# Differential attention with a quantised gate: where the exponentials are kept, the order of maxima and combination, and the steps of the gate product

## The chip, the cores and the metric

The kernel runs on one core of one Trainium2 chip. The metric is the device time of one execution in microseconds. Engine names are those of the profile: PE is TensorE (PEld its weight loads), DVE is VectorE, ACT is ScalarE, POOL is GpSimd, SP is SyncE, whose queue issues all transfers here.

## The reference, cut to what matters

The input is x of shape (8, 512, 512). It is normalised, and two things are computed from it: a differential attention with 8 pairs of query heads over 4 pairs of key heads, and a gate, which is SiLU of a product whose operands are rounded to a 4-bit block format. The output is x + attention * gate.

```python
xn = layernorm(x)
q, k, v = split(xn @ Wqkv.T + b)            # 16 q heads, 8 k heads of 128; 4 v of 256
p = softmax_causal(q1 k1) - lam * softmax_causal(q2 k2)
o = (p @ v) * rsqrt(mean((p @ v)**2) + eps) * subln_w * (1 - lambda_init)
s = o @ out_w.T + out_b
g = silu(quant(xn) @ quant(W_ffn).T + b_ffn)
x = x + s * g
```

## The kernel before

**Steps.** After a setup (weights transposed and split) the kernel goes through 8 batches (b) of 512 tokens, each in 32 steps (s); n = 32 b + s counts all 256. A step is one pair of query heads on one block of 128 tokens, with w = 128, 256, 384 or 512 keys: s % 8 = 0, 1 have 128; 2, 3 have 256; 4, 5 have 384; 6, 7 have 512. Eight steps share a group g of keys and values. Every product is made of three matmuls on float16 pairs (a high part and a remainder), so each result is split by two operations: ACT writes the high part, DVE the remainder.

**A step's own chain.** `scores(n)` on PE (6 matmuls of w columns) fills two rows of PSUM, m = 1 and m = 0. `maxima(n, m)` on DVE scales and masks a row in place and gives its bound. `exps(n)` on ACT takes the two exponentials: that of m = 1 stays in PSUM, that of m = 0 goes to `pp` in SBUF. `combine(n)` on DVE (reciprocal, coefficient, product) forms p in PSUM; `p_hi(n)` on ACT and `p_lo(n)` on DVE write `ph`; `transpose_p(n)` on SP's queue turns it into `pT` by a DMA transpose; `attend(n)` on PE multiplies by v. Then `square_o` (ACT), `norm_of` (POOL), `normalised` (ACT), `normalised_lo` (DVE) and `transpose_o` (SP) bring the head into `heads`.

**Fills.** Between `scores(n + 2)` and `attend(n)` PE computes what `PLAN[n]` lists: a projection q, k (12 matmuls of 512 columns) or v (24 of 256), the output product "out" of the batch before (48 of 512, in steps 1, 3, 5, 7), and the gate product "ffn" (4 of 512, in steps 10 to 13). Two PSUM banks hold them in turn (`fill_free` returns a bank). A q or k fill is split by ACT, then DVE (L658, L940); a v fill goes DVE (L946), ACT (L663), POOL (`v_low`, L1138); an ffn fill DVE (L952), ACT's tanh (L669), POOL (`gating`, L1150 and L1152). In the last batch the output product of its own first two blocks is cut in pieces ("last"), from step 22 on, which hold one bank.

**Order.** Each engine's program is an order written by hand: one iteration n per step. The iteration of each engine does:

- PE: `scores(n + 2)`, the fills of n, `attend(n)`.
- DVE: `combine(n + 1)`, `maxima(n + 2, 1)`, `p_lo(n + 1)`, `maxima(n + 2, 0)`, `normalised_lo(n - 1)`, the fills of n.
- ACT: `square_o(n - 1)`, `p_hi(n + 1)`, `normalised(n - 1)`, `exps(n + 2)`, the fills of n.
- SP: `transpose_p(n + 1)`, loads and the transposes of x (`X_TURN`, steps 21 and 22) and of the quantised x, `transpose_o(n - 1)`.

`scores(n)` may overwrite a pair of rows when `p_lo(n - 2)` has read it:

```python
wait(pe, ph_lo, n - 1)
```

In steps with `X_SPLIT` ACT and DVE also split a block of the next batch's x. In the steps after an "out" fill DVE does the maxima last.

Of the kernel before, what the change touches and what calls it, by code (L numbers as in the profile page):

```python
# [7 lines left out]
F32 = mybir.dt.float32  # L8
# [12 lines left out]
G = 4  # L21
# [19 lines left out]
PH = 4 - AHEAD  # L41
# [10 lines left out]
FFN_STEP = 10  # L52
# [17 lines left out]
def schedule(has_prev, has_next):  # L70

    steps = [[] for _ in range(NS)]
    for g in (1, 2, 3):

        at = (None, PROJ_AT, PROJ_AT[:6] + (7, 8), (0, 1, 1, 2, 3, 3, 4, 5))[g]
        for s, (kind, j) in zip(at, PROJ):
            steps[(g - 1) * STEPS + s].append((kind, g, j))
    for k in range(NT):
        if has_prev:
            steps[2 * k + 1].append(("out", 0, k))  # L80

        steps[FFN_STEP + k].append(("ffn", 0, k))
# [4 lines left out]
    else:  # L87
# [9 lines left out]
X_SPLIT = {15: 0, 17: 1, 18: 2, 19: 3}  # L97
# [78 lines left out]
def build(nc, x_d, wqkv_d, bqkv_d, lq1_d, lk1_d, lq2_d, lk2_d, sub_d, ow_d, ob_d, fw_d, fb_d, out_d):  # L176
# [4 lines left out]
    with ctx:  # L181
# [22 lines left out]
        pp = sb("pp", [P, S], F32)  # L204
# [3 lines left out]
        junk = sb("junk", [P, E], BF16)  # L208
# [10 lines left out]
        lam4, lam2 = pp, v32[:, 1, :]  # L219
# [46 lines left out]
        ld_bias = sem("ld_bias")  # L266
        ld_w = [sem(f"ld_w{n}") for n in range(16)]
# [43 lines left out]
        tanh_one = sem("tanh_one")  # L311
        gate_done = sem("gate_done")
# [54 lines left out]
        def _(sp):  # L367
# [65 lines left out]
            for n in range(NSTEPS):  # L433
# [18 lines left out]
                if s == 0 and b:  # L452
                    sp.wait_ge(xT_done[1], 16 * (b + 1))
# [29 lines left out]
        def _(pe):  # L483
# [48 lines left out]
            def scores(n):  # L532
# [6 lines left out]
                wait(pe, ph_lo, n - 1)  # L539
# [27 lines left out]
            for kind, n in setup_order():  # L567
# [20 lines left out]
                for c in range(4):  # L588
                    last = tr(setup_bank(m)[:, c * P:(c + 1) * P], slot(kind, n // 2)[:, n % 2, c * P:(c + 1) * P], ident[:])
# [20 lines left out]
        def _(act):  # L610
# [42 lines left out]
            def fill(f):  # L653
# [17 lines left out]
            def exps(n):  # L671
                u, w = n % 2, place(n)[3]

                wait(act, eps_done, n - 5)
                for a, m in enumerate((1, 0)):
                    act.wait_ge(max_done, 2 * n + a + 1)
                    sc = sc_ps[u][:, m, 0:w]
                    if m == 0:

                        wait(act, comb_done, n)  # L680
                    run(sc if m else pp[:, 0:w], sc, ACT.Exp, bias=ebias[:, u, m:m + 1], scale=-1.0,  # L681
                        accum_out=psum_l[:, n % 6, m:m + 1]).then_inc(exp_done, 1)

            def p_hi(n):
# [5 lines left out]
                run(ph[:, n % PH, 0:w], sc_ps[u][:, 1, 0:w], ACT.Copy, scale=sigma).then_inc(ph_hi, 1)  # L690
# [539 lines left out]
```

## Time and profile before

| | us |
|---|---|
| median of 3 runs | 1753.76 (1753.6 to 1755.99) |
| the profiled execution's own time | 1754.4 |
| its span, first to last instruction | 1752.6 |
| PE busy in the span | 1538.7 (88%) |
| DVE, ACT, POOL busy | 1196.0 (68%), 885.8 (51%), 662.4 (38%) |
| batch 5, from the end of the last attend of batch 4 to that of batch 5 | 200.48 |

The span is split below by the ends of `attend(n)` on PE. Matmuls overlap, and a matmul's printed duration is longer than the time from its start to that of the next; so the length of a stretch says more than PE's busy share in it. Of a pair of rows on one engine, the distance of the starts is the time that the first one takes from the engine. "PEclk" is the clock granted to PE as a share of the full one. An idle time in brackets is that of the engine just before the row, with what ended it.

### The profile page before, as it was taken

What the parts mean: (1) busy time and instruction counts of PE and PEld (TensorE: products, weight loads), DVE (VectorE), ACT (ScalarE), POOL (GpSimd) and SP (SyncE); (2) the same over time, 40 slices, a digit from 0 to 9 for tenths busy, and PEclk for the clock granted to TensorE, in tenths of its full rate; (3) what the DMA queues carried; (4) which work ended last, traced back from release to release, by engine and by line L of the source; (5) the groups of instructions that cost most, each with busy time, mean ns of one, the idle gap of its engine ahead of it and who ended that gap; (6) DMA issues with size and microseconds to landing.
All of it is one profiled execution on the core that took longest, in us unless ns stands there. A gap on an engine that the chain in (4) does not pass through costs nothing. (4 is left out here: it accounts for less than half of the span.)

```text
span 1752.6 us, 28521 instructions
## 1 busy us (share of the span) xinstructions
PE 1538.7 (88%) x9137; PEld 899.8 (51%) x9153; DVE 1196.0 (68%) x3177; ACT 885.8 (51%) x2542; POOL 662.4 (38%) x1161
## 2 busy tenths in 40 slices
PE   2666588999989988999889988999989989899898
PEld 1343355555555555545555555545555546555554
DVE  4467777776777677776677667775777767675682
ACT  4563356535663456535664356634564356533561
POOL 2103542345324443344424443244424443243433
PEclk7778799999999999999999999999999999999999
DMA  7401334333342334333352334324342333422433
GB/s 250 140 4 27 64 67 82 61 88 70 50 91 55 84 73 82 64 78 72 55 87 57 84 73 79 68 46 100 55 85 54 95 63 65 80 54 67 64 76 73
DMA packets 385353, 130.63 MB, mean 75 GB/s; under 512 B 366354, under 2 KB 366900, under 8 KB 385204
## 3 DMA queue, kind: packets, MB, share of 16 engines
q1 hardware_dynamic: 385204, 128.81, 35.4%
q8 instruction: 73, 1.20, 0.3%
q14 instruction: 76, 0.62, 0.1%
HBM read 31.74 MB, written 8.39 MB: 23 GB/s over the span
## 5 line engine op out<-in xcount | busy, mean ns | idle before, releaser
L690 ACT ACTIVATE ph<-ps,small 128x128 f16<-128x128 f32 (+3 forms) x256 | 134.4, 525 | 395.0 <-DVE ps L981 394.4
L1168 POOL TENSOR_SCALAR norm<-psum_l,small 128x1 f32<-128x1 f32 x256 | 88.4, 345 | 584.9 <-ACT pp L681 584.9
L970 DVE CUSTOM_DVE_ANT_0 ps<-ps,mask,ssc 128x384 f32<-128x384 f32 (+3 forms) x512 | 279.7, 551 | 35.9 <-PE ps L547 35.4
L490 PE MATMUL ps<-xT,wqkv 128*128 128x512 f16 x768 | 297.6, 387 | 6.8 <-DVE qkv L940 6.4
L491 PE MATMUL ps<-xT,wqkv 128*128 128x512 f16 x768 | 296.4, 386 | 0.0
L492 PE MATMUL ps<-xT,wqkv 128*128 128x512 f16 x768 | 295.5, 385 | 0.0
L940 DVE SCALAR_TENSOR_TENSOR qkv<-ps,bsc,qkv 128x512 f16<-128x512 f32 x192 | 143.3, 750 | 187.0 <-ACT qkv L658 187.0
L490 PE MATMUL ps<-qkv,pT 128*128 128x256 f16 x640 | 179.6, 281 | 74.3 <-DMA pT<-ph 73.5
L545 PE MATMUL ps<-qkv 128*128 128x384 f16 (+3 forms) x512 | 155.2, 309 | 56.5 <-DVE ph L987 53.6
L490 PE MATMUL ps<-wout,heads 128*128 128x512 f16 x512 | 194.1, 379 | 0.5 <-DVE small L956 0.5
L491 PE MATMUL ps<-wout,heads 128*128 128x512 f16 x512 | 194.0, 379 | 0.0
L492 PE MATMUL ps<-wout,heads 128*128 128x512 f16 x512 | 194.0, 379 | 0.0
L987 DVE SCALAR_TENSOR_TENSOR ph<-ps,small,ph 128x128 f16<-128x128 f32 (+3 forms) x256 | 141.0, 551 | 77.2 <-ACT ph L690 68.6
L702 ACT ACTIVATE on<-ps,norm 128x256 f16<-128x256 f32 x256 | 120.5, 471 | 132.7 <-POOL norm L1176 130.0
L492 PE MATMUL ps<-qkv,pT 128*128 128x256 f16 x640 | 180.3, 282 | 0.0
L491 PE MATMUL ps<-qkv,pT 128*128 128x256 f16 x640 | 179.7, 281 | 0.0
L993 DVE SCALAR_TENSOR_TENSOR on<-ps,norm,on 128x256 f16<-128x256 f32 x256 | 123.1, 481 | 66.8 <-ACT on L702 66.5
L1174 POOL TENSOR_TENSOR var<-norm,sumsq 128x1 f32<-128x1 f32 x256 | 65.1, 254 | 246.7 <-ACT junk L694 246.6
L546 PE MATMUL ps<-qkv 128*128 128x384 f16 (+3 forms) x512 | 155.4, 309 | 0.0
L547 PE MATMUL ps<-qkv 128*128 128x384 f16 (+3 forms) x512 | 155.3, 309 | 0.0
L681 ACT ACTIVATE pp<-ps,ebias 128x128 f32<-128x128 f32 (+3 forms) x256 | 135.0, 527 | 37.0 <-DVE ebias L970 35.9
L1176 POOL TENSOR_TENSOR norm<-var,small 128x1 f32<-128x1 f32 x256 | 143.6, 561 | 20.0
(147 smaller groups left out, 3146.9 us busy)
## 6 DMA issues: line engine op xcount, KB each, us to landing
xin<-in_L_attn_hidden_states SPq DMA_DIRECT2D x8, 1024.0 KB, 5.8
xres<-in_L_attn_hidden_states SPq DMA_DIRECT2D x32, 256.0 KB, 2.8
out_x<-res SPq DMA_DIRECT2D x32, 256.0 KB, 2.4
qkv<-in_L_attn_Wqkv_w SPq DMA_DIRECT2D x8, 512.0 KB, 7.3
heads<-in_L_attn_Wqkv_w SPq DMA_DIRECT2D x8, 512.0 KB, 10.7
pT<-ph SPq DMA_TRANSPOSE x256, 2.7
heads<-on SPq DMA_TRANSPOSE x256, 2.5
qkv<-in_L_attn_out_w SPq DMA_DIRECT2D x4, 512.0 KB, 5.6
```

The lines of the kernel that those rows point to most:

```text
L490: mm(out, ah, bh, start=start and j == 0, stop=False)
L491: mm(out, ah, bl, start=False, stop=False)
L492: last = mm(out, al, bh, start=False, stop=stop and j == n - 1)
L545: mm(out, qh, k[:, 0, m, 0:w], start=True, stop=False)
L546: mm(out, qh, k[:, 1, m, 0:w], start=False, stop=False)
L547: last = mm(out, ql, k[:, 0, m, 0:w], start=False, stop=True)
L681: run(sc if m else pp[:, 0:w], sc, ACT.Exp, bias=ebias[:, u, m:m + 1], scale=-1.0, accum_out=psum_l[:, n % 6, m:m + 1]).then_inc(exp_done, 1)
L690: run(ph[:, n % PH, 0:w], sc_ps[u][:, 1, 0:w], ACT.Copy, scale=sigma).then_inc(ph_hi, 1)
L940: stt(out=dst(kind, g, j, 1), in0=bank, scalar=bsc[:, g, c:c + 1], in1=dst(kind, g, j, 0), op0=ALU.add, op1=ALU.subtract).then_inc(fill_fr ...
L970: nc.vector.tensor_tensor_reduce(sc, sc, mask[:, S - w:S], ssc[:, c:c + 1], BIG, ALU.add, ALU.min, ebias[:, u, m:m + 1]).then_inc(max_done, 1)
L987: stt(out=ph[:, n % PH, w:2 * w], in0=sc_ps[u][:, 1, 0:w], scalar=sigma, in1=ph[:, n % PH, 0:w], op0=ALU.mult, op1=ALU.subtract).then_inc( ...
L1176: pt(nr[:, 1:2], var[:], minushalf, ALU.pow).then_inc(norm_done, 1)
```

## The change

- The exponential of m = 1 goes to SBUF as well: `pp` has three slices, 0 for m = 0 and 1 + n % 2 for m = 1. `combine` reads two slices and writes one, all in SBUF; `p_hi` and `p_lo` read SBUF. `scores(n)` waits for the two exponentials of step n - 2 instead of for `p_lo(n - 2)`.
- DVE does both maxima of step n + 2, then `combine(n + 1)` and `p_lo(n + 1)`. ACT does the exponential of m = 1 of step n + 2 ahead of `p_hi(n + 1)`, that of m = 0 after `normalised(n - 1)`. Steps after an "out" fill keep combination, remainder, fill, maxima on DVE.
- The ffn fills go from steps 10 to 13 to steps 22 to 25 and stand last in their step. DVE adds the bias in PSUM (`biased`), ACT takes the tanh out of PSUM into `gate`, and in its next iteration DVE (`gating`, one operation of 512 columns) multiplies, which returns the bank. POOL's two operations for it go.
- The two v fills of group 2 go from steps 15 and 16 to steps 14 and 15. The first split of the next batch's x goes from steps 15 and 17 to 14 and 16; its halves are kept in `gate` instead of `res`, `xres` and `aq`. The transposes of the quantised x stay at steps 10 and 11.
- The bias of v is loaded for each group in turn (a DMA of 256 floats to all partitions at every eighth step) instead of once, and its scale is applied in the fill: a scalar_tensor_tensor in place of a tensor_tensor.
- The junk output of `square_o` goes to PSUM. In the last batch SP loads the first residual after step 25 instead of 22.

```diff
-FFN_STEP = 10
+FFN_STEP = 22
-        at = (None, PROJ_AT, PROJ_AT[:6] + (7, 8), (0, 1, 1, 2, 3, 3, 4, 5))[g]
+        at = (None, PROJ_AT, PROJ_AT, (0, 1, 1, 2, 3, 3, 4, 5))[g]
...
-X_SPLIT = {15: 0, 17: 1, 18: 2, 19: 3}
+X_SPLIT = {14: 0, 16: 1, 18: 2, 19: 3}
...
+                if n and s % STEPS == 0 and n // STEPS + 1 < G * B:
+                    load_v(n // STEPS + 1)
...
-                wait(pe, ph_lo, n - 1)
+                wait(pe, exp_done, 2 * n - 2)
...
-                    act.wait_ge(fill_free, n + 1)
-                    wait(act, gate_done, f.gate)
-                    wait(act, v_lo, f.v)
-                    run(t2, gate[:, j, :], ACT.Tanh, scale=0.5).then_inc(tanh_done, 1)
+                    act.wait_ge(biased, f.gate + 1)
+                    wait(act, gated, f.gate - NT + 1)
+                    if f.gate // NT + 1 < B:
+                        act.wait_ge(xT_done[j], 16 * (f.gate // NT + 2))
+                    run(gate[:, j, :], bank, ACT.Tanh, scale=0.5).then_inc(tanh_done, 1)
...
+                if n + AHEAD < NSTEPS and not late:
+                    exps(n + AHEAD, 1)
                 if n + AHEAD - 1 < NSTEPS:
                     p_hi(n + AHEAD - 1)
...
-                stt(out=sc_ps[u][:, 1, 0:w], in0=sc_ps[u][:, 1, 0:w], scalar=coef[:, u:u + 1], in1=pp[:, 0:w],
+                stt(out=pp[:, 1 + u, 0:w], in0=pp[:, 1 + u, 0:w], scalar=coef[:, u:u + 1], in1=pp[:, 0, 0:w],
...
+            def gating(f):
+                dve.wait_ge(tanh_done, f.gate + 1)
+                stt(out=gate[:, f.j, :], in0=gate[:, f.j, :], scalar=1.0, in1=fbank[f.bank], op0=ALU.add, op1=ALU.mult)\
+                    .then_inc(fill_free, 1)
...
+                if n + AHEAD < NSTEPS and not late:
+                    maxima(n + AHEAD, 1)
+                if n + AHEAD < NSTEPS and not late:
+                    maxima(n + AHEAD, 0)
                 if n + AHEAD - 1 < NSTEPS:
                     combine(n + AHEAD - 1)
-                if n + AHEAD < NSTEPS and not late:
-                    maxima(n + AHEAD, 1)
-                if n + AHEAD - 1 < NSTEPS:
                     p_lo(n + AHEAD - 1)
...
+                for f in PLAN[n - 1] if n else ():
+                    if f.kind == "ffn":
+                        gating(f)
```

## Rows read from the trace of the kernel before

**Rows 1.** Waits of PE after the setup, 180 us to the end: us in total, times, longest.
```profile
PE ps L490 <- DMA pT<-ph: 73.5, 36, 3.9
PE ps L545 <- DVE ph L987: 37.7, 25, 11.4
```
**Rows 2.** Batch 5 by stage (steps 0-7, 8-13, 14-16, 17-21, 22-24, 25-31), from the view by windows.
```profile
1132.56:1207.86 75.30, 75.30 (x423) 40.63 (x421) 50.50 (x126) 27.68 (x77) 35.34 (x53) 1.00 0.31 70
1207.86:1238.71 30.85, 29.17 (x161) 15.35 (x162) 22.32 (x58) 18.78 (x54) 13.15 (x23) 1.00 0.36 76
1238.71:1257.05 18.34, 14.89 (x107) 11.16 (x105) 11.45 (x33) 10.23 (x32) 9.86 (x16) 0.81 0.37 58
1257.05:1284.24 27.19, 27.16 (x174) 16.68 (x173) 22.32 (x56) 17.74 (x49) 8.00 (x16) 1.00 0.27 50
1284.24:1298.99 14.75, 9.00 (x59) 5.80 (x57) 7.98 (x28) 7.81 (x29) 4.71 (x11) 0.88 0.77 143
1298.99:1333.04 34.05, 31.23 (x210) 19.29 (x208) 26.02 (x72) 20.77 (x63) 8.59 (x22) 1.00 0.40 65
```
**Rows 3.** The same view for step 9 of batch 5 alone.
```profile
1211.43:1215.00 3.57, 3.57 (x23) 2.00 (x21) 2.98 (x9) 1.72 (x6) 2.90 (x4) 1.00 0.20 41
```
**Rows 4.** DVE in order of time, one step of 512 keys with a q fill.
```profile
1319.22 0.15 DVE L977 RECIPROCAL recip<-psum_l 128x1 f32<-128x1 f32 x1
...
1320.38 0.75 DVE L970 CUSTOM_DVE_ANT_0 ps<-ps,mask,ssc 128x512 f32<-128x512 f32 x1
...
1321.23 0.75 DVE L987 SCALAR_TENSOR_TENSOR ph<-ps,small,ph 128x512 f16<-128x512 f32 x1
1321.90 0.75 DVE L970 CUSTOM_DVE_ANT_0 ps<-ps,mask,ssc 128x512 f32<-128x512 f32 x1
...
1324.13 0.75 DVE L940 SCALAR_TENSOR_TENSOR qkv<-ps,bsc,qkv 128x512 f16<-128x512 f32 x1 [1.09 <-ACT qkv L658]
1324.80 0.15 DVE L977 RECIPROCAL recip<-psum_l 128x1 f32<-128x1 f32 x1
```
**Rows 5.** ACT in the same step.
```profile
1320.51 0.69 ACT L690 ACTIVATE ph<-ps,small 128x512 f16<-128x512 f32 x1 [1.63 <-DVE ps L981]
1321.10 0.47 ACT L702 ACTIVATE on<-ps,norm 128x256 f16<-128x256 f32 x1
...
1322.74 0.69 ACT L681 ACTIVATE pp<-ps,ebias 128x512 f32<-128x512 f32 x1 [0.51 <-DVE ebias L970]
...
1323.42 0.68 ACT L658 ACTIVATE qkv<-ps,bsc 128x512 f16<-128x512 f32 x1
```
**Rows 6.** ACT in step 13 of batch 5, which has an ffn fill.
```profile
1235.55 0.63 ACT L669 ACTIVATE v<-gate 128x512 f32<-128x512 f32 x1 [2.30 <-DVE gate L952]
...
1236.45 0.68 ACT L690 ACTIVATE ph<-ps,small 128x512 f16<-128x512 f32 x1
```
**Rows 7.** A DVE split that reads SBUF alone, grouped by form: busy us, mean ns.
```profile
L1007 DVE SCALAR_TENSOR_TENSOR aq<-xin,aq 128x512 f16<-128x512 f32 x16 | 10.8, 682 | 0.0
```
**Rows 8.** DVE in order of time, two maxima in a row.
```profile
1151.08 0.62 DVE L970 CUSTOM_DVE_ANT_0 ps<-ps,mask,ssc 128x384 f32<-128x384 f32 x1 [0.51 <-PE ps L547]
...
1151.63 0.62 DVE L970 CUSTOM_DVE_ANT_0 ps<-ps,mask,ssc 128x384 f32<-128x384 f32 x1
```
**Rows 9.** DVE in order of time, the form of rows 7 in batch 2.
```profile
652.84 1.23 DVE L1007 SCALAR_TENSOR_TENSOR res<-xin,res 128x512 f16<-128x512 f32 x1 [1.21 <-ACT res L711]
```
**Rows 10.** POOL in the same stretch.
```profile
652.37 1.16 POOL L1138 TENSOR_TENSOR qkv<-v,qkv 128x512 f16<-128x512 f32 x1 [0.71 <-ACT qkv L663]
```
**Rows 11.** Issues of SP's queue, steps 22 and 23 of batch 5.
```profile
1288.49 1.26 SPq L410 DMA_TRANSPOSE pT<-ph  x1
...
1293.95 1.20 SPq L410 DMA_TRANSPOSE pT<-ph  x1
```
**Rows 12.** The transposes of p (L410) in steps 8 to 31 of batch 5, from issue to landing.
```profile
DMA to landing us min/median/max: 2.3/2.6/4.5
```

More of the change, by code:

```diff
@@ L40 @@
 AHEAD = 2
-PH = 4 - AHEAD
+PH = 2
 ROUND = (22 << 23) + (1 << 22)
@@ L92, in schedule @@
             steps[LAST_STEP + s].insert(0, ("last", p, k))
+    for k in range(NT):
+        steps[FFN_STEP + k].append(("ffn", 0, k))
     return steps
 PROLOGUE = [(kind, 0, j) for kind, j in PROJ]
-X_SPLIT = {15: 0, 17: 1, 18: 2, 19: 3}
+X_SPLIT = {14: 0, 16: 1, 18: 2, 19: 3}
 X_TURN = {21: (0, 1), 22: (2, 3)}
@@ L266, in build @@
         ld_bias = sem("ld_bias")
+        ld_vb = [sem(f"ld_vb{u}") for u in range(2)]
         ld_w = [sem(f"ld_w{n}") for n in range(16)]
@@ L396, in _ @@
                 load_w(n)
+            for k in range(NT):
+                sp.wait_ge(xT_done[k], 16)
             sp.dma_start(gate[:], fw_d.rearrange("(k p) h -> p k h", p=P)).then_inc(ld_fw, 16)
@@ L458, in _ @@
                         residual(b - 1, (s - 1) // 2)
-                if b == B - 1 and s == LAST_STEP:
+                if b == B - 1 and s == FFN_STEP + 3:
+                    sp.wait_ge(fill_done, fill_of("ffn", b, 0, 1) + 1)
                     residual(b, 0)
-                for k in {FFN_STEP - 1: (0, 1), FFN_STEP: (2, 3)}.get(s, ()):
+                for k in {10: (0, 1), 11: (2, 3)}.get(s, ()):
                     if k == 0:
@@ L664, in fill, with exps @@
                 elif kind == "ffn":
[L666 to L682 removed]
+                    act.wait_ge(biased, f.gate + 1)
[3 more added lines that the diff above has]
+                    run(gate[:, j, :], bank, ACT.Tanh, scale=0.5).then_inc(tanh_done, 1)
+            def exps(n, m):
+                u, w = n % 2, place(n)[3]
+                if m:
+                    wait(act, eps_done, n - 5)
+                    wait(act, ph_lo, n - 1)
+                else:
+                    wait(act, comb_done, n)
+                act.wait_ge(max_done, 2 * n + 2 - m)
+                out = pp[:, 1 + u, 0:w] if m else pp[:, 0, 0:w]
+                run(out, sc_ps[u][:, m, 0:w], ACT.Exp, bias=ebias[:, u, m:m + 1], scale=-1.0,
+                    accum_out=psum_l[:, n % 6, m:m + 1]).then_inc(exp_done, 1)
             def p_hi(n):
@@ L944, in fill @@
                     wait(dve, v_lo, f.v)
-                    wait(dve, gate_done, f.ffn)
-                    tt(v32[:], bank.rearrange("p (a e) -> p a e", a=2),
-                       vbias[:, g, :].unsqueeze(1).broadcast_to([P, 2, E]), ALU.add).then_inc(fill_free, 1)
+                    t = f.v // 2
+                    dve.wait_ge(ld_vb[t % 2], 16 * (t // 2 + 1))
+                    stt(out=v32[:], in0=vbias[:, t % 2, :].unsqueeze(1).broadcast_to([P, 2, E]), scalar=vscale[:, g:g + 1],
+                        in1=bank.rearrange("p (a e) -> p a e", a=2), op0=ALU.mult, op1=ALU.add).then_inc(fill_free, 1)
                 elif kind == "ffn":
                     dve.wait_ge(fill_done, n + 1)
-                    wait(dve, gated, f.gate - NT + 1)
-                    tt(gate[:, j, :], bank, fbias[:], ALU.add).then_inc(fill_free, 1)
+                    tt(bank, bank, fbias[:], ALU.add).then_inc(biased, 1)
                 elif kind == "last" and LAST_PIECES[j][g][1] < OC:
@@ L1056, in _ @@
                     fill(f)
-                if n + AHEAD < NSTEPS:
-                    if late:
-                        maxima(n + AHEAD, 1)
+                if n + AHEAD < NSTEPS and late:
+                    maxima(n + AHEAD, 1)
                     maxima(n + AHEAD, 0)
+                for f in PLAN[n - 1] if n else ():
+                    if f.kind == "ffn":
+                        gating(f)
                 prepare(b, s, "maxima")
@@ L1145, in _ @@
             v_low(0, 1, 1)
-            def gating(f):
-                pool.wait_ge(tanh_done, f.gate + 1)
-                pt(t2, t2, one.broadcast_to([P, HID]), ALU.add).then_inc(tanh_one, 1)
-                pool.wait_ge(tanh_one, f.gate + 1)
-                pt(gate[:, f.j, :], t2, gate[:, f.j, :], ALU.mult).then_inc(gate_done, 1)
             def finish(f):
@@ L1186, in _ @@
                 for f in PLAN[n - 1] if n else ():
-                    if f.kind == "ffn":
-                        gating(f)
-                    elif f.kind == "out" or f.kind == "last" and LAST_PIECES[f.j][f.g][1] == OC:
+                    if f.kind == "out" or f.kind == "last" and LAST_PIECES[f.j][f.g][1] == OC:
                         finish(f)
```

64 lines of the change are left out of this document (35 added, 29 removed).

## The prediction

> **What bounds the kernel now.** I read PE's waits first, to see which ones are worth anything, then the stages of one batch, then the order of time on DVE and ACT. PE is the engine with the most work, and behind the setup it waits for two things above all: transposed tiles p that land late (73.5 us) and `p_lo`, which frees the rows of the scores (37.7) [rows 1]. Step 9 shows what PE needs when it waits for nothing: 6 score matmuls, 24 halves of a k fill and 3 of attend, 33 units of 256 columns in 3.57 us, 0.108 each [rows 3]. By that unit the stages of a batch [rows 2] compare with their bare PE work so:
>
> - steps 0 to 7: 75.3 us without a gap; output products cover everything. What an engine does here costs nothing.
> - 8 to 13: 266 units, 28.8, took 30.85.
> - 14 to 16: 111 units, 12.0, took 18.34, at 0.81 of the clock: PE idled for 3.5 us and then ran part of the stage at the lower of its two levels.
> - 17 to 21: 249 units, 26.9, took 27.19: PE-bound.
> - 22 to 24: 63 units, 6.8, took 14.75.
> - 25 to 31: 279 units, 30.2, took 34.05.
>
> So 20 us of a batch of 200 are not PE's work. They stand where fills are thin (14, 22, 23) or where a loop through DVE and ACT is longer than PE's step. That loop can be read off one step [rows 4, 5]. Combination starts at 1319.22; p_hi starts at 1320.51, p_lo at 1321.23, the second maximum at 1321.90, its exponential 1322.74, the q fill's high part 1323.42, its remainder 1324.13, the next combination 1324.80: 5.58 us, against PE's 45 units (4.9). The first maximum lies under p_hi for nothing; the second is in the loop.
>
> **The loop after.** Both maxima come first. Two in a row start 0.55 apart at 384 columns [rows 8], so 0.67 each at 512, where a like DVE row takes 0.67 [rows 4]. Combination: 1.26 from its start to its end (1320.48, by p_hi's start less 0.03). Its operands are in SBUF then; the nearest row is a split reading SBUF alone, 0.682 [rows 7] against 0.75 for the PSUM one [rows 4], so I take 1.19. A bound from below is this, from above no gain, 1.26. p_hi to normalised 0.59, less about 0.05 for an SBUF source (the tanh out of SBUF takes 0.63, p_hi 0.68 [rows 6]): 0.54. Normalised to the exponential 0.36, as now to the first one, exponential to fill 0.68, to remainder 0.71, remainder 0.67 [rows 4, 5]. Sum 1.34 + 1.19 + 0.03 + 0.54 + 0.36 + 0.68 + 0.71 + 0.67 = 5.52 against 5.58. The maximum that was hidden is paid for (+0.67), but p_lo and the second maximum's wait leave the loop. Each 128 keys fewer take about 0.12 from each of five operations, 0.6, from either loop. So in steps with a q or k fill the new order by itself is worth about nothing. In steps with a v fill ACT's tail isn't in the loop and p_hi's wait, now uncovered, is: I count 4.9 at 512 keys and 4.5 at 384/512, about 0.5 more than before.
>
> **The gate product leaves steps 10 to 13.** Its bias (0.6 us of DVE) stood at the end of the loop and its tanh on ACT stood ahead of p_hi: it starts at 1235.55, p_hi only at 1236.45 behind it and the square [rows 6], so most of its 0.63 is in the loop too: 5.58 + 0.6 + 0.6 = 6.8 at 512 keys. After: loops of 4.3, 4.7, 4.9, 5.3 and 5.5 from step 9 on, beginning 4.7 us after the end of step 7 in both kernels (the k fill of step 8 sets it). Counting from the end of step 7, PE's work of 234 units is done at 25.3; p of step 13 is written 22.1 and lands 24.9, just late: stage 25.9 against 30.85, **-5.0**.
>
> **The v fills one step earlier.** Step 14 has work then. Loop 13 starts at 23.8, p of 14 lands 31.0 (4 us to p_lo's end, 3.2 transpose), PE is ready at 28.8: it idles 2.2 instead of 3.5, too short, I take it, for the clock to fall. p of 15 lands at 35.7, step 15 ends 37.0, step 16 (a single k) 40.6: 14.7 against 18.34, **-3.6**.
>
> **Steps 17 to 21.** The DVE loops (5.0, 5.3, 6.2, 4.5, 4.9 with splits of x and double fills) sum to 25.9, PE's work is 26.9. Bare PE work and 0.6 of waits: 27.5, **+0.3**.
>
> **Steps 22 to 24.** Three ffn fills add 24 units (2.6) where PE idles anyway, but the loops get ffn bias (0.6) and gating (0.67), and bank reuse now runs through DVE: an ffn fill waits for the gating of the one before, which stands behind the maxima, combination and p_lo. Counting on: step 21 ends 68.1; p of 22 lands 72.4, step 22 ends 73.8; p of 23 lands 77.8, since combination waits for `v_low` (next part), and step 23 ends 79.6 with some slow clock. Maxima start on the scores of 26 at 80.3, gating ends 83.2, ffn fill 84.1, step 24 ends 84.5, and tanh ahead of p_hi costs 0.5: 16.9 against 14.75, **+2.2**. SP is no better off: its two issues of p stand 5.46 apart here [rows 11], with four others between, and it gets one more short load at steps 8, 16 and 24, at most one transposing issue of 1.26, behind the transpose of p.
>
> **Steps 25 to 31.** One more ffn fill and gating at 25, q loops as before, v loops at the end 0.5 longer: step 31 ends 34.4 later against 34.05, **+0.4**. Sum -5.7 a batch.
>
> **Late landings.** I used 2.4 to 3.3 us for a transpose; they take up to 4.5 [rows 12], and at steps without slack that is lost. The old stages hold some such losses, the new ones need them too: **+1.5** a batch, one at the largest. So -4.2 a batch.
>
> **The shared path of DVE and POOL.** A DVE split of two SBUF operands took 1.23 instead of 0.68 when POOL's `v_low` had begun 0.47 before it; it ended 0.5 behind it [rows 7, 9, 10]. Before, combination had one operand in PSUM; after, combination and p_lo have two in SBUF. `v_low` comes after DVE's v operation (0.68, like the others) and ACT's high part (0.63, like the tanh) with two hops, so it starts about 0.75 after the next loop's start and ends at 1.9; combination's long part comes at 1.0 (128 keys) to 1.8 (512). So 0.6 to 0.9 is lost in the loops of 16 and 22 (in the sums above), after step 31 there is slack. The Trainium skill has the same rule ("SBUF — State Buffer", section "SBUF: two separate sides"): a DVE operation with two SBUF inputs and a GpSimd operation lock each other out for a whole instruction. It speaks against this change; the row agrees with it, 1.23 against 0.68. The other small POOL operations (0.2 to 0.6) fall under the maxima, by the loop's timing.
>
> **First and last batch, setup.** Batch 0 has no output products: in steps 0 to 8 DVE sets the pace and the uncovered p_hi wait (0.3 to 0.7) less what SBUF operands save costs it about 0.45 a step, +4, against the 4.2 that the later steps win: nothing. Batch 7: the pieces hold one bank, so every ffn fill waits for the gating of the one before it. A step is then scores (0.65), maxima, combination, p_hi and p_lo (2.2), gating (0.7), ffn fill (0.9) and attend: about 5 each in 23 to 25 where PE has 2 to 3 of work. That gives back all that 8 to 21 gain there (8.3) and a little more, by an estimate **+1.4**. Setup and tail: nothing but a smaller bias load.
>
> **Sum.** 6 x -4.2 + 1.4 = -23.8. The profiled execution took 1754.4, so 1730.6; the median of before is 0.6 under it: **1730**. Own range of this case 1714 to 1744.
>
> **Rivals.**
>
> - *The lead is given back* (0.20). p lands late at steps 14, 22 and 23, each by the full 1.9 between median and largest landing [rows 12]: 5.7 a batch, all that is won. For it: PE's longest waits end on these landings [rows 1], and DVE is late at 22. Against: the same chance existed before. Time 1754 + 1.4, 1755; this case spreads over 1748 to 1760.
> - *Slower by the shared path* (0.12). If not only `v_low` but POOL's short operations too hold combination or p_lo, say 0.56 in each of the 22 loops of steps 9 to 30, that is 12.3 a batch against 5.7 won: +6.6 in seven batches, 1800. It decides from 0.26 us a loop. By the skill's rule as written every GpSimd operation that reads SBUF could do it; only their timing, under the maxima, speaks against.
> - *More than I count* (0.08). With bare PE work in steps 8 to 21 and no late landing, -8.4 a batch and no loss after: 1754 - 55, 1699.
> - That the change does nothing because PE's wait for `p_lo` only turns into one for a landing: it holds in 25 to 31, and is in the sums.
>
> **Chances.** The forecast 0.60. Faster by over 0.2% (3.5 us, about what a measurement of this kernel can tell) 0.75, within it 0.08, slower 0.17. The range reaches from the edge of the better case to the equal one: 1708 to 1757.
>
> **What would show it.** In a batch: no DVE-caused waits of PE at 10 to 13; loops of 5.5 us at 512 keys; steps 14 to 16 in 14.7 at a clock near 1.0; steps 22 to 24 longer than before; DVE rows of the combination at 0.69 (512), some at over 1.2 beside `v_low`. The prediction is wrong if combinations are long without `v_low`, or if 17 to 21 is no longer PE-bound.

## The result: slower, 1783.07 us

| | before | after |
|---|---|---|
| median of 4 runs each, us | 1753.68 | 1783.07 |
| ratio, 95% interval | | 1.0173, 1.0151 to 1.0195 |
| profiled execution: its time, its span | 1754.4, 1752.6 | 1787.4, 1785.5 |
| PE, DVE, POOL busy | 1538.7, 1196.0, 662.4 | 1541.0, 1246.8, 604.3 |

The forecast was 1730 with a range of 1708 to 1757. The kernel is 29 us slower, outside of the range, where 24 us faster was forecast. The two spans differ by 32.9: setup -0.8, batch 0 +2.6, batches 1 to 6 together +19, batch 7 +12.2.

One correction to the description of the change: the transposes of the quantised x stood at steps 9 and 10 before (`FFN_STEP - 1` and `FFN_STEP`) and stand at 10 and 11 after. They move by one step.

The view by windows of the kernel after, batch 5 by the same six stages as [rows 2]:

```profile
1146.13:1223.14 77.01, 75.63 (x422) 40.38 (x421) 54.66 (x128) 27.61 (x78) 36.34 (x54) 1.00 0.29 72
1223.14:1251.14 28.00, 26.00 (x148) 13.80 (x146) 20.27 (x55) 17.01 (x50) 8.77 (x19) 1.00 0.46 88
1251.14:1268.69 17.55, 13.73 (x107) 10.54 (x105) 11.89 (x34) 10.55 (x33) 5.51 (x11) 0.90 0.40 57
1268.69:1295.67 26.98, 26.98 (x174) 16.72 (x173) 21.09 (x54) 17.66 (x48) 7.86 (x16) 1.00 0.28 57
1295.67:1313.55 17.88, 11.53 (x70) 6.66 (x69) 13.12 (x36) 10.17 (x32) 5.15 (x12) 0.90 0.78 119
1313.55:1350.32 36.77, 33.30 (x213) 20.79 (x212) 27.68 (x74) 22.43 (x65) 8.66 (x22) 0.95 0.32 64
```

Means over batches 1 to 6, from the ends of `attend`, for this kernel and for two of the experiments below:

| steps | before | after | change | predicted | old order | p_lo last |
|---|---|---|---|---|---|---|
| 0-7 | 75.3 | 76.5 | +1.2 | 0 | 75.8 | 75.3 |
| 8-13 | 30.9 | 28.1 | -2.7 | -5.0 | 26.3 | 26.7 |
| 14-16 | 18.1 | 16.2 | -1.9 | -3.6 | 16.0 | 13.4 |
| 17-21 | 27.0 | 28.0 | +1.0 | +0.3 | 28.2 | 27.6 |
| 22-24 | 14.4 | 17.4 | +3.0 | +2.2 | 16.0 | 15.9 |
| 25-31 | 34.1 | 36.7 | +2.6 | +0.4 | 35.1 | 33.1 |

So the gains in 8 to 16 exist but are about half of what was counted, and stages forecast at nothing lose. PE's waits after the setup (us in total, times, longest) say on what:

```profile
PE ps L504 <- DMA pT<-ph: 96.3, 64, 4.8
PE ps L529 <- DVE gate L985: 14.4, 11, 3.0
PE ps L504 <- DVE on L1017: 13.4, 2, 11.7
```

Against [rows 1] the wait for `p_lo` is gone (37.7), the one for landings grew from 73.5 in 36 times to 96.3 in 64, and an ffn fill's wait for a bank is new. One step shows how. DVE in order of time, 512 keys with a q fill, the iteration n = 29 as in [rows 4]:

```profile
1334.85 0.75 DVE L959 SCALAR_TENSOR_TENSOR qkv<-ps,bsc,qkv 128x512 f16<-128x512 f32 x1 [0.59 <-ACT qkv L672]
1335.52 0.75 DVE L994 CUSTOM_DVE_ANT_0 ps<-ps,mask,ssc 128x512 f32<-128x512 f32 x1
...
1336.18 0.76 DVE L994 CUSTOM_DVE_ANT_0 ps<-ps,mask,ssc 128x512 f32<-128x512 f32 x1
...
1336.85 0.16 DVE L1001 RECIPROCAL recip<-psum_l 128x1 f32<-128x1 f32 x1
...
1337.37 0.75 DVE L1005 SCALAR_TENSOR_TENSOR pp<-pp,coef 128x512 f32<-128x512 f32 x1
1338.91 0.75 DVE L1011 SCALAR_TENSOR_TENSOR ph<-pp,small,ph 128x512 f16<-128x512 f32 x1 [0.79 <-ACT ph L704]
...
1340.52 0.75 DVE L959 SCALAR_TENSOR_TENSOR qkv<-ps,bsc,qkv 128x512 f16<-128x512 f32 x1 [0.46 <-ACT qkv L672]
```

ACT in the same step:

```profile
1338.15 0.72 ACT L704 ACTIVATE ph<-pp,small 128x512 f16<-128x512 f32 x1 [0.93 <-DVE pp L1005]
1338.78 0.46 ACT L716 ACTIVATE on<-ps,norm 128x256 f16<-128x256 f32 x1
1339.13 0.68 ACT L695 ACTIVATE pp<-ps,ebias 128x512 f32<-128x512 f32 x1
1339.80 0.68 ACT L672 ACTIVATE qkv<-ps,bsc 128x512 f16<-128x512 f32 x1
```

From remainder to remainder the loop is 1340.52 - 1334.85 = 5.67, 0.1 longer than in [rows 4]. But `p_lo` starts 4.06 behind the remainder (1338.91 - 1334.85); before it was 2.68 by the same count over all batches (2.01 behind combination's start in [rows 4], and the remainder another 0.67 ahead). SP's transpose of p and the attend of that p, n = 30, first in the kernel after (SP's queue, then PE):

```profile
1339.68 1.23 SPq L422 DMA_TRANSPOSE pT<-ph  x1
...
1343.01 0.39 PE L504 MATMUL ps<-qkv,pT 128*128 128x256 f16 x1 [2.20 <-DMA pT<-ph]
```

The same two of the kernel before:

```profile
1322.01 1.23 SPq L410 DMA_TRANSPOSE pT<-ph  x1
...
1325.30 0.28 PE L490 MATMUL ps<-qkv,pT 128*128 128x256 f16 x1
```

Issue to attend is 3.3 in both. Before, PE came to this attend from a fill without a pause; after, it stood for 2.2 us until p had landed, and then worked at the lower of its two clock levels for a while: the matmuls of this attend start 0.21 apart, those of the kernel before 0.11.

### The profile page after: what moved, and what is told of

The parts are those of the page before. It is cut to its first block, busy times and chain, and to the rows that moved or that the text cites. A ratio compares the mean times of both kernels' runs of the same rounds, so it can differ in the third digit from the quotient of the medians.

```text
span 1785.5 us, 28499 instructions
## 1 busy us (share of the span) xinstructions
PE 1541.0 (86%) x9137; PEld 899.8 (50%) x9153; DVE 1246.8 (70%) x3209; ACT 897.0 (50%) x2542; POOL 604.3 (34%) x1097
## 4 chain that ended last, share of the span: by engine, by line
DVE 38%; PE 17%; ACT 14%; issue 10%; POOL 10%; DMA 6%; SPq 1%; POOLq 0%; ACTq 0%; DVEq 0%
DVE ps L994 9%; DVE pp L1005 6%; DVE qkv L959 5%; PE ps L504 5%; PE ps L506 5%; PE ps L505 4%; ACT pp L695 4%; ACT qkv L672 4%; DMA pT<-ph 3%; ACT ph L704 3%; ACT on L716 3%; DVE coef L1003 3%; DVE ph L1011 2%; POOL qkv L1165 2%; DVE aq L844 1%
## 5 line engine op out<-in xcount | busy, mean ns | idle before, releaser
L695 ACT ACTIVATE pp<-ps,ebias 128x384 f32<-128x384 f32 (+3 forms) x512 | 266.6, 521 | 306.4 <-DVE ebias L994 306.2
L504 PE MATMUL ps<-xT,wqkv 128*128 128x512 f16 x768 | 294.0, 383 | 8.8 <-DMA xT<-gate 4.9
L504 PE MATMUL ps<-qkv,pT 128*128 128x256 f16 x640 | 183.3, 286 | 135.3 <-DMA pT<-ph 113.6
L704 ACT ACTIVATE ph<-pp,small 128x128 f16<-128x128 f32 (+3 forms) x256 | 143.6, 561 | 308.0 <-DVE pp L1005 307.9
L505 PE MATMUL ps<-xT,wqkv 128*128 128x512 f16 x768 | 293.4, 382 | 0.0
L506 PE MATMUL ps<-xT,wqkv 128*128 128x512 f16 x768 | 293.0, 382 | 0.0
L994 DVE CUSTOM_DVE_ANT_0 ps<-ps,mask,ssc 128x384 f32<-128x384 f32 (+3 forms) x512 | 262.1, 553 | 42.2 <-PE ps L561 41.7
L1011 DVE SCALAR_TENSOR_TENSOR ph<-pp,small,ph 128x128 f16<-128x128 f32 (+3 forms) x256 | 147.9, 578 | 184.6 <-ACT ph L704 184.5
L506 PE MATMUL ps<-qkv,pT 128*128 128x256 f16 x640 | 183.8, 287 | 0.0
L505 PE MATMUL ps<-qkv,pT 128*128 128x256 f16 x640 | 183.3, 286 | 0.0
L1005 DVE SCALAR_TENSOR_TENSOR pp<-pp,coef 128x128 f32<-128x128 f32 (+3 forms) x256 | 174.9, 683 | 9.0
L504 PEld LDWEIGHTS ps<-qkv,pT 128*128 128x128 f16 x640 | 64.7, 101 | 198.5 <-DMA pT<-ph 156.0
L1194 POOL TENSOR_TENSOR var<-norm,sumsq 128x1 f32<-128x1 f32 x256 | 77.1, 301 | 235.1 <-ACT ps L708 235.0
```

Source lines behind the costliest of these rows:

```text
L504: mm(out, ah, bh, start=start and j == 0, stop=False)
L505: mm(out, ah, bl, start=False, stop=False)
L506: last = mm(out, al, bh, start=False, stop=stop and j == n - 1)
L695: run(out, sc_ps[u][:, m, 0:w], ACT.Exp, bias=ebias[:, u, m:m + 1], scale=-1.0, accum_out=psum_l[:, n % 6, m:m + 1]).then_inc(exp_done, 1)
L704: run(ph[:, n % PH, 0:w], pp[:, 1 + u, 0:w], ACT.Copy, scale=sigma).then_inc(ph_hi, 1)
L994: nc.vector.tensor_tensor_reduce(sc, sc, mask[:, S - w:S], ssc[:, c:c + 1], BIG, ALU.add, ALU.min, ebias[:, u, m:m + 1]).then_inc(max_done, 1)
```

## The experiments

The theories at the start: **A**, the new order of DVE and ACT costs the time; **B**, DVE and POOL hold each other up over their shared path, now that combination reads and writes SBUF; **C**, the gate product at steps 22 to 25 costs more than it gives back. All medians are in us, and each ratio is to the kernel before, run in the same group on the same chip. The median of that kernel was 1756.9, 1754.4, 1755.3 and 1755.8 in the four groups of experiments and 1753.7 beside the kernel after. So a difference between kernels of different groups is uncertain by about 3 us, and one of under 5 us does not settle much.

**The order back.** The kernel after with DVE's and ACT's order of before. Edits of order are shown in this section with their conditions left out.

```diff
-                    maxima(n + AHEAD, 1); maxima(n + AHEAD, 0)
-                    combine(n + AHEAD - 1); p_lo(n + AHEAD - 1)
+                    combine(n + AHEAD - 1); maxima(n + AHEAD, 1)
+                    p_lo(n + AHEAD - 1); maxima(n + AHEAD, 0)
...
-                    exps(n + AHEAD, 1)
                     p_hi(n + AHEAD - 1)
                     normalised(n - 1)
+                    exps(n + AHEAD, 1)
                     exps(n + AHEAD, 0)
```

> The changed kernel with one part undone: DVE again does combination, first maximum, remainder, second maximum, and ACT both exponentials behind the normalised head. Exponentials stay in SBUF, the gate product stays at steps 22 to 25. The changed kernel takes 1783, before 1754. Theory A (order: the wait of the combination behind both maxima and the uncovered wait for p_hi are what costs, about 0.15 to 0.5 us in each DVE loop): 1755 to 1767. Theory B (lock: combination and remainder with two SBUF operands stop for GpSimd, 40 us of added DVE time in the trace after): stays 1775 to 1785. Theory C (the gate product at 22 to 25 holds up PE through the gating on DVE): stays 1775 to 1785, with steps 22 to 25 as long as now.

1734.85 against 1756.92, ratio 0.9873 (0.9850 to 0.9897), better than theory A itself had expected. The order alone accounts for 48 us; without it the change is a gain of 22. PE's waits in it:

```profile
PE ps L504 <- DMA pT<-ph: 78.4, 50, 5.2
```

All waits of PE after the first 180 us sum to 152 us in the kernel after and to 119 here. By the record of PE's clock over the same stretch it stood at the lower level for 94 us there and for 64 here; 30 us at half speed are up to 15 us lost, by estimate. The 34 of waits and these 15 make up nearly all of the 49.8 us between the two spans.

**Exponentials back in PSUM.** The kernel after; the scores wait for `p_lo` again.

```diff
-                wait(pe, exp_done, 2 * n - 2)
+                wait(pe, ph_lo, n - 1)
...
-                out = pp[:, 1 + u, 0:w] if m else pp[:, 0, 0:w]
+                out = sc_ps[u][:, 1, 0:w] if m else pp[:, 0, 0:w]
...
-                stt(out=pp[:, 1 + u, 0:w], in0=pp[:, 1 + u, 0:w], ...
+                stt(out=sc_ps[u][:, 1, 0:w], in0=sc_ps[u][:, 1, 0:w], ...
```

> The changed kernel with the exponential of m = 1, the combination and p back in PSUM (scores wait for the remainder again), the new order and the gate product at 22 to 25 kept. Theory B (lock): the combination has one SBUF operand again, no row of it above its free length, 1762 to 1772. Theory A (order) and theory C (gate product): 1778 to 1786, since nothing of either is touched.

1778.27, ratio 1.0123 (1.0103 to 1.0142): 5 us under the kernel after, or 8 when each is set against the kernel before of its own group. No combination is held up in this kernel. Those of 512 keys by form (busy us, mean ns):

```profile
L1004 DVE SCALAR_TENSOR_TENSOR ps<-ps,coef,pp 128x512 f32<-128x512 f32 x64 | 48.6, 759 | 2.3
```

So theory B is at most a small part of the loss, and most of it is still there without it.

**The gate product back at 10 to 13**, with the fills of v and the splits of x (steps and tiles) as before, once in the new and once in the old order.

```diff
-FFN_STEP = 22
+FFN_STEP = 10
-X_SPLIT = {14: 0, 16: 1, 18: 2, 19: 3}
+X_SPLIT = {15: 0, 17: 1, 18: 2, 19: 3}
```

> The changed kernel with the gate product back at steps 10 to 13 and the v fills of group 2 and the splits of x at their old steps; bias in PSUM and gating on DVE, the new order and the exponentials in SBUF kept. Theory C: batch 7 gets back the 18 us that it loses in steps 22 to 31 of the trace after, and the other batches some 4 in 22 to 31, less 4.6 that they win in 8 to 16: 1762 to 1770. Theory A: the order costs more where the loop also carries bias and gating, 1780 to 1790. Theory B: about 1780.

> The changed kernel with both undone: old order on DVE and ACT, gate product at 10 to 13. What is left of the change is exponentials in SBUF, gating on DVE out of PSUM, the load of v's bias by group. If order and gate product are the whole loss (A and C): 1750 to 1758. If the lock is most of it (B): 1768 to 1780.

1902.93 (ratio 1.0835, 1.0812 to 1.0857) and 1779.76 (1.0141, 1.0110 to 1.0173). The first is over 110 us above every theory's expectation. Neither reads cleanly, since the transposes of the quantised x were left at steps 10 and 11, behind the fill that needs them. PE's waits in the first of them:

```profile
PE ps L529 <- DVE gate L983: 49.6, 24, 2.3
...
PE ps L529 <- DMA xres<-aq: 46.3, 6, 9.2
```

**The same with these transposes at 9 and 10, as before.**

```diff
-                for k in {10: (0, 1), 11: (2, 3)}.get(s, ()):
+                for k in {9: (0, 1), 10: (2, 3)}.get(s, ()):
```

> The changed kernel with the gate product at steps 10 to 13 and the transposes of the quantised x back at steps 9 and 10, new order. Without the 46 us of waits for these transposes, if they were time lost on PE: 1845 to 1865. If the order costs the same 48 us wherever the gate product stands: the other of this pair plus 48. If a loop that also carries bias and gating makes the late p_lo dearer: plus 60 to 90.

> The same with the old order. If gating on VectorE and the rest cost nothing against the kernel before, 1750 to 1760. If each gate fill waits for the gating of the one before (49.6 us of PE's waits in the new order's trace): 1765 to 1778. Against the old order with the gate product at 22 to 25 (1735) it gives the gain of the steps.

1854.18 in the new order (1.0559, 1.0525 to 1.0593) and 1744.97 in the old one (0.9939, 0.9922 to 0.9957), the second below both of its expectations. Moving the gate product to 22 to 25, together with the v fills and the splits of x, gains 71 us in the new order and 10 in the old. C falls. PE's waits in the first:

```profile
PE ps L504 <- DMA pT<-ph: 96.9, 47, 4.8
PE ps L529 <- DVE gate L983: 48.7, 24, 2.3
PE ps L529 <- DMA xres<-aq: 19.3, 7, 4.8
```

**Why is the order dear?** Two forms of A were put against each other: A1, `p_lo` comes later because two maxima stand ahead of it; A2, DVE's wait for p_hi, which nothing covers now, is lost DVE time. Three kernels change the order alone. The first puts the maximum of m = 0 back behind `p_lo`:

```diff
                     maxima(n + AHEAD, 1)
-                    maxima(n + AHEAD, 0)
                     combine(n + AHEAD - 1)
                     p_lo(n + AHEAD - 1)
+                    maxima(n + AHEAD, 0)
```

> The changed kernel with the maximum of m = 0 back behind p_lo; that of m = 1 stays ahead of the combination, ACT unchanged. Theory A1 (phase): the DVE loop is as long in both orders, 5.67 us at 512 keys, and what costs 48 us is that the combination, and with it p_lo and the landing of p, come two maxima (1.1 to 1.3 us) later in each loop, in the steps where attend waits for p. Then one maximum costs half: 1755 to 1764. Theory A2 (the uncovered wait of DVE for p_hi is the cost, as a loss of DVE time): nothing covers it here either, 1775 to 1785.

1827.85, ratio 1.0427 (1.0404 to 1.0449): 45 us worse than the kernel after, and far above what either form expected (1755 to 1764 and 1775 to 1785). A1 as stated, in which each maximum ahead of `p_lo` has its price, falls, and so does A2. The place of `p_lo` did come 0.67 earlier, but the second maximum went back into the loop, now 6.35 long.

The second takes ACT's order of before and leaves DVE's new:

> The changed kernel with ACT's old order alone (p_hi, normalised head, both exponentials); DVE does both maxima ahead of the combination. The exponential of m = 1 comes into the loop, 0.33 to 0.66 us a step. Theory A1: p_lo's place in the loop doesn't move, but the loop gets longer: slower than the changed kernel by 10 to 50 us, 1795 to 1830, mostly in steps 8 to 13 and 25 to 31. Theory A2 (DVE's time): DVE has the same work and waits, 1780 to 1788.

1835.10, ratio 1.0466 (1.0448 to 1.0485), just above A1's 1795 to 1830 for a longer loop and 47 us above A2's upper bound, with the same operations and waits on DVE. `p_lo` stands at 4.06 as in the kernel after; the exponential that stood under combination is in the loop, 6.33 long.

The third takes ACT's order of before and on DVE combination, both maxima, `p_lo`, so that the maxima lie under the wait for p_hi:

```diff
-                    maxima(n + AHEAD, 1); maxima(n + AHEAD, 0)
-                    combine(n + AHEAD - 1); p_lo(n + AHEAD - 1)
+                    combine(n + AHEAD - 1)
+                    maxima(n + AHEAD, 1); maxima(n + AHEAD, 0)
+                    p_lo(n + AHEAD - 1)
```

> The changed kernel with ACT's old order and, on DVE, combination, both maxima, then p_lo. Both maxima lie under p_hi and the normalised head, so p_lo waits for nothing and the second maximum leaves the loop: by the rows the loop at 512 keys is 1.26 + 0.03 + 0.62 + 0.36 + 0.66 + 0.68 + 0.71 + 0.67 = 5.0 us instead of 5.67, while p_lo comes 0.6 us later in it than in the old order. Theory A1 with phase as the larger part: 1738 to 1750, slower than the old order's 1735. If the length of the loop is the larger part: 1718 to 1730.

**1690.69, ratio 0.9638 (0.9624 to 0.9653)**, the fastest kernel here, and 27 us below the better of its two expectations: the direction was foreseen for a shorter loop, its size was not. DVE in it, from remainder to remainder at 512 keys:

```profile
1270.69 0.75 DVE L956 SCALAR_TENSOR_TENSOR qkv<-ps,bsc,qkv 128x512 f16<-128x512 f32 x1 [0.69 <-ACT qkv L672]
1271.36 0.15 DVE L998 RECIPROCAL recip<-psum_l 128x1 f32<-128x1 f32 x1
...
1272.52 0.75 DVE L991 CUSTOM_DVE_ANT_0 ps<-ps,mask,ssc 128x512 f32<-128x512 f32 x1
...
1273.19 0.76 DVE L991 CUSTOM_DVE_ANT_0 ps<-ps,mask,ssc 128x512 f32<-128x512 f32 x1
...
1273.86 0.75 DVE L1008 SCALAR_TENSOR_TENSOR ph<-pp,small,ph 128x512 f16<-128x512 f32 x1
...
1275.67 0.75 DVE L956 SCALAR_TENSOR_TENSOR qkv<-ps,bsc,qkv 128x512 f16<-128x512 f32 x1 [0.67 <-ACT qkv L672]
```

ACT in it:

```profile
1272.64 0.72 ACT L704 ACTIVATE ph<-pp,small 128x512 f16<-128x512 f32 x1 [1.60 <-DVE pp L1002]
1273.27 0.46 ACT L716 ACTIVATE on<-ps,norm 128x256 f16<-128x256 f32 x1
1273.62 0.68 ACT L695 ACTIVATE pp<-ps,ebias 128x512 f32<-128x512 f32 x1
...
1274.29 0.68 ACT L695 ACTIVATE pp<-ps,ebias 128x512 f32<-128x512 f32 x1
...
1274.95 0.69 ACT L672 ACTIVATE qkv<-ps,bsc 128x512 f16<-128x512 f32 x1
```

The loop is 4.98 and no maximum is in it: the chain is combination, p_hi, normalised, two exponentials, the fill's high part, its remainder. `p_lo` waits for nothing and starts at 3.17. PE's waits (us, times, longest):

```profile
PE ps L504 <- DMA pT<-ph: 55.5, 43, 4.0
...
PE ps L529 <- DVE gate L982: 8.5, 10, 2.0
```

**Old order and PSUM**, both undone; what is left is the gate product's steps and its form, the earlier v fills and the bias loads.

> The changed kernel with the old order on DVE and ACT and with the exponential of m = 1, combination and p in PSUM: what is left of the change is the gate product at steps 22 to 25 with gating on DVE, the early v fills and small parts. If exponentials in SBUF help by freeing the rows of the scores early (PE waited 37.7 us for p_lo before): slower than the old order's 1735, 1740 to 1750. If the lock between VectorE and GpSimd costs more than that gives: 1725 to 1733. With the new order PSUM was 5 us faster (1778 against 1783).

1727.99, ratio 0.9849 (0.9834 to 0.9864). These parts are worth -26 us. SBUF costs 7 in the old order (4 when each is set against its own kernel before), and the new order costs 50 with p in PSUM (1778.27 against 1727.99), as much as with p in SBUF. PE's waits in old_psum:

```profile
PE ps L504 <- DMA pT<-ph: 45.4, 30, 2.7
PE ps L559 <- DVE ph L1007: 44.1, 41, 11.4
```

With SBUF, in old_order, the 44.1 are gone and the wait for landings is 78.4 instead of 45.4: three quarters of the wait for `p_lo` came back as one for its transfer.

**p_lo last in PSUM, and in the kernel before.**

> The order combination, both maxima, p_lo, with the exponential of m = 1, combination and p back in PSUM. With SBUF it took 1691. Both theories that stand (the length of the loop, 5.0 us at 512 keys, and the place of p_lo in it) give the same loop; the lock between VectorE and GpSimd is gone: 1681 to 1688. If freeing the rows of the scores early is worth more with p_lo this late in the loop: 1692 to 1700.

> The kernel before with one edit: DVE does combination, both maxima, p_lo. Gate product at steps 10 to 13, gating on GpSimd, exponentials as before. The loop loses 0.6 us at 512 keys (the second maximum): in steps 8 to 16 and 22 to 31. If that loop is what binds it there, as in the changed kernel: 44 us as there, 1705 to 1720. If the gate product at 10 to 13 and the thin step 14 bind it: 1725 to 1745.

1695.15 (0.9654, 0.9638 to 0.9671) and 1735.80 (0.9892, 0.9871 to 0.9912). With this order SBUF seems to gain 4.5, but the intervals of the two ratios overlap, so the sign is not settled. The order alone gives 20 us in the kernel before and 33 in old_psum's.

**The place alone.** In place of A1 stands now: the time follows both the loop's length and the place of `p_lo` in it. This kernel changes the place only: in p_lo last, `p_lo` goes behind `normalised_lo`.

```diff
                     maxima(n + AHEAD, 0)
-                    p_lo(n + AHEAD - 1)
...
                     normalised_lo(n - 1)
+                    p_lo(n + AHEAD - 1)
```

> The order combination, both maxima, p_lo with exponentials in SBUF (1691), with p_lo another 0.4 us later, behind the remainder of the normalised head. ACT sets the loop, so it stays at 5.0 us at 512 keys; only p_lo's place moves. If that place has a price of its own, as 1.35 us made 48 us between the old and the new order: 1700 to 1710. If only the length of the loop counts: 1689 to 1694.

1708.57, ratio 0.9733 (0.9716 to 0.9749). The loop stays at 4.98, `p_lo` starts 0.40 later, and that alone costs 18 us.

**The last batch's gate product at 16 to 19**, in p_lo last in PSUM.

```diff
-        steps[FFN_STEP + k].append(("ffn", 0, k))
+        steps[(FFN_STEP if has_next else 16) + k].append(("ffn", 0, k))
```

> As p in PSUM with the order combination, maxima, p_lo, and in the last batch alone the gate product at steps 16 to 19 instead of 22 to 25, where the pieces of the output product hold one bank. If the wait of each gate fill for the gating of the one before is what lengthens the last batch: 3 to 6 us faster than the same kernel without it, 1677 to 1684. If steps 22 to 25 of the last batch are set by the landings alone: within 1 us of it.

1696.25 (0.9661, 0.9645 to 0.9677) against 1695.15 in the same group: no difference.

**The new order alone in the kernel before**, on DVE and ACT.

> The kernel before with the new order on VectorE and ScalarE alone: both maxima, combination, p_lo, and the exponential of m = 1 ahead of p_hi; gate product at 10 to 13, gating on GpSimd, p in PSUM. Loop length theory: the loop is as long as before (5.58 at 512 keys), so nothing, 1750 to 1760. Place theory: p_lo comes 1.35 us later in the loop and p lands later in every step without slack, as in the changed kernel, 40 to 55 us: 1795 to 1810.

1795.90, ratio 1.0230 (1.0213 to 1.0247). The order costs 40 us there too. Its waits of PE:

```profile
PE ps L490 <- DMA pT<-ph: 81.0, 41, 4.6
PE ps L545 <- DVE ph L991: 60.6, 78, 11.5
```

In this kernel the scores still wait for `p_lo`: that wait grew from 37.7 to 60.6. In the kernel after it can't, since the scores wait for exponentials; the lateness comes out at the landings instead.

The kernels by the loop at n = 29 (512 keys, a q fill) and by the place of `p_lo` in it, behind the remainder that starts it (medians of batches 1 to 6). Times compare within a block; the two columns are measured in this one step and serve as a mark of the order.

| kernel | loop | p_lo at | median |
|---|---|---|---|
| *gate product at 22 to 25, SBUF* | | | |
| p_lo_last | 4.98 | 3.17 | 1690.7 |
| p_lo_later | 4.98 | 3.57 | 1708.6 |
| old_order | 5.67 | 2.71 | 1734.9 |
| after | 5.67 | 4.06 | 1783.1 |
| one_ahead | 6.35 | 3.39 | 1827.9 |
| act_old | 6.33 | 4.06 | 1835.1 |
| *gate product at 22 to 25, PSUM* | | | |
| p_lo_last_psum | 4.96 | 3.17 | 1695.2 |
| old_psum | 5.64 | 2.68 | 1728.0 |
| in_psum | 5.64 | 4.03 | 1778.3 |
| *gate product at 10 to 13, product on DVE, SBUF* | | | |
| ffn10_old_order | 5.67 | 2.71 | 1745.0 |
| ffn10_new_order | 5.67 | 4.06 | 1854.2 |
| *gate product at 10 to 13, product on POOL, PSUM* | | | |
| before_p_lo_last | 4.96 | 3.17 | 1735.8 |
| before | 5.58 | 2.68 | 1755.8 |
| before_new_order | 5.64 | 4.03 | 1795.9 |

In every block a later place at nearly equal length is slower: 0.40 costs 18 us, and about 1.35 costs 48, 50, 109 and 40. The one run that moves nothing but `p_lo` is p_lo_later. At an equal place 0.66 more of loop costs 52 (after, act_old). In the longest loops the place matters less (6.35 and 6.33: 7 us for 0.67). Where the two columns moved in opposite directions (one_ahead against after, the kernels with `p_lo` last against those of the old order), the length won.

## Why the prediction was wrong

**The step that failed** is the verdict on the loop: "in steps with a q or k fill the new order by itself is worth about nothing". Its sum was nearly right, 5.52 against a measured 5.67, and old_order has the same 5.67, so the length is indeed worth nothing. But the sum went from remainder to remainder and left out where in it p is handed over. `p_lo` went from 2.7 to 4.06 because both maxima, 1.34, were put ahead of the chain combination, p_hi, `p_lo`, transpose, landing, attend. The prediction walked the landings of single steps (13, 14, 15, 22, 23); for the others it had only its term for late landings, +1.5 a batch, which is the spread of the transposes and has nothing to do with when p is handed over. Between old_order and the kernel after, with nothing else changed, the order is 48 us.

With it taken out the change gives 1735, inside the forecast range, but that is in part luck. In old_order's trace a batch of 1 to 6 gains 2.5 where 4.2 was forecast, and setup and batch 0 gain 4.1 where nothing was.

**No slack for a later p.** In the kernel before, attend(30) starts with no idle time 3.3 behind the issue; in the kernel after the same attend waits 2.2. The 37.7 us that PE waited for `p_lo` [rows 1] were a sign that `p_lo` is late as it is. The prediction's last rival says that this wait may turn into one for a landing in steps 25 to 31, and puts it "in the sums", where these steps have +0.4; they lost 2.6.

**The terms of the loop.** Combination was put at 1.19 and p_hi to normalised at 0.54, both less than before, for an SBUF source. The groups by form of the kernel after (busy us, mean ns) deny both:

```profile
L1005 DVE SCALAR_TENSOR_TENSOR pp<-pp,coef 128x512 f32<-128x512 f32 x64 | 54.9, 858 | 2.3
...
L704 ACT ACTIVATE ph<-pp,small 128x512 f16<-128x512 f32 x64 | 46.2, 722 | 68.1 <-DVE pp L1005 68.1
```

Undisturbed, combination is 0.75 as it was in PSUM, and in the row at 1338.15 p_hi takes ACT for 0.63 until normalised. Its length, 722 ns, is above the 685 of before, not below. The 682 of [rows 7] is of an operation whose scalar is a constant; whether that is the difference was not tried.

**The gains.** Steps 8 to 13 were forecast at 25.9, old_order has 26.3: right, with the order out of the way. With it 28.1: the attends of steps 10 to 13 wait 2.1 for p, 0.6 in old_order. The loop of step 9 took 5.1 where 4.3 was counted, but it takes 4.9 in old_order too, so it is not the difference. One part of it stands in batch 5: POOL was still finishing the last output product; combination took 0.70 beside it, and POOL's small operation after that 0.37 where 0.19 is its least. POOL in order of time:

```profile
1228.79 1.27 POOL L1180 TENSOR_TENSOR res<-res,xres 128x512 f32<-128x512 f32 x1
1230.02 0.37 POOL L1194 TENSOR_TENSOR var<-norm,sumsq 128x1 f32<-128x1 f32 x1
```

DVE beside it, 256 keys, where this width took 0.49 on average in the kernel before:

```profile
1229.64 0.70 DVE L1005 SCALAR_TENSOR_TENSOR pp<-pp,coef 128x256 f32<-128x256 f32 x1
```

Steps 14 to 16 were forecast at 14.7; 16.2 came, 13.4 with `p_lo` last. Steps 22 to 24 at +2.2 came at +3.0 and 17 to 21 at +0.3 came at +1.0. Steps 25 to 31 at +0.4 came at +2.6: with the old order they lost 0.9, and in p_lo_last the stage is 33.1, under the kernel before.

**The shared path.** The mechanism was right and is to be seen in step 22. DVE, then POOL:

```profile
1298.56 1.48 DVE L1005 SCALAR_TENSOR_TENSOR pp<-pp,coef 128x512 f32<-128x512 f32 x1
```

```profile
1298.34 1.15 POOL L1165 TENSOR_TENSOR qkv<-v,qkv 128x512 f16<-128x512 f32 x1 [1.04 <-ACT qkv L677]
1299.45 0.64 POOL L1194 TENSOR_TENSOR var<-norm,sumsq 128x1 f32<-128x1 f32 x1
```

Combination took 1.48 where 0.75 is usual. The Trainium skill has this as a lock for a whole instruction ("SBUF — State Buffer", section "SBUF: two separate sides"), and the trace agrees, 1.48 against 0.75. But the rival built on it, 1800 from 0.56 us a loop, did not bring the loss, although its number is nearer than the forecast's. By form, combination and `p_lo` together keep DVE busy for 323 us in the kernel after, 318 in old_order and 284 with p in PSUM. So the shared path costs nearly the same DVE time in either order, 39 and 34 us, spread over other operations; and with p in PSUM, where it costs nothing, the order still costs 50. The prediction was wrong about who holds combination up: of 52 long ones in the kernel after 23 lie beside `v_low` and 29 beside POOL's long operations on the residual and on the next x (1.27 us each), none beside the short ones. Long combinations without `v_low` were its own sign of being wrong.

**Batch 7** was put at +1.4 and lost 12.2; in old_order it lost 2.1, so the order has most of this as well. The forecast had the mechanism, an ffn fill that waits for gating while the pieces hold one bank; PE in steps 22 to 24 of batch 7:

```profile
1710.38 1.02 PE L529 MATMUL ps<-wffn,xres 128*128 128x512 bf16 x4 [1.95 <-DVE gate L985]
...
1718.69 1.49 PE L529 MATMUL ps<-wffn,res 128*128 128x512 bf16 x3 [3.01 <-DVE small L974]
```

The first wait ended on gating (L985), the second by the trace on the small operation behind it that returns a piece (L974). These three steps took 21.7 where they had taken 9.2; they took 16.2 in old_order and 13.7 in p_lo_last. In p_lo_last_psum moving the last batch's gate product gave nothing. What the bank costs in the kernel after by itself is open.

**Sum.** Measured parts of the +29: gate product, v fills and loads -26, SBUF +7, order +48. These are differences of medians from several groups, each good to about 3 us. The forecast's -24 is close to the first part alone, which is chance, since it was meant for the whole; it put the third at nothing.

A side sum does not come out: the third rival's -8.4 a batch. Bare PE work in steps 8 to 21 is 25.3 + 12.0 + 26.9 = 64.2 against the 68.1 counted, which makes -9.6. The forecast does not use it.

**Left open.** Why SBUF costs 5 to 7 in two orders and about nothing, or less, in the third: it frees the scores' rows early and meets POOL more, and the two weren't separated. Why the same later place costs 109 us with the gate product at 10 to 13 on DVE and 40 to 50 elsewhere. How much of the -26 is the product on DVE and how much the steps: ffn10_old_order, with SBUF in, is 11 under before, and the move is another 10.

## What to carry to other kernels

In a loop through several engines count two numbers: its length, and how far behind its start the result that another engine waits for is handed over. An operation that leaves the loop's length as it is can still delay the hand-over if it is put ahead of it; put it where the engine waits anyway (here both maxima under p_hi: 1690.7 instead of 1783.1 from the same operations). A wait for an operation that is also the source of a transfer is a warning about the transfer: between old_psum and old_order such a wait of 44 us was removed, the wait for the transfer grew by 33, and nothing was gained.

## What the runs showed of the hardware

- Two operands in SBUF instead of one in PSUM did not shorten DVE's combination: 752 ns at 512 columns against 759. On ACT the scaled copy became longer out of SBUF, 722 against 685.
- POOL's operation on a single column, 0.19 at best, took 0.64 beside a combination out of SBUF that itself took 1.48 instead of 0.75.
- DVE's second maximum (512 columns) starts 0.66 behind the first, and the reading of the first's accumulator, 0.14, starts at the same moment: the read lies under the next operation.
